# Two waits on GpSimd in a two-layer decoder: when the padded keys are zeroed, and when projection weights are split

## The reference, cut to what matters

```python
x = ln(x + hgrn(x, Wi, Wf, Wg, Wo, g_norm))                      # phase A
x = ln(x + cross_attention_one_head(x, ctx))                     # phase B
x = ln(x + experts_top2_of_8_width_64(x))                        # phase C
x = ln(x + causal_self_attention_16_heads(x, Wq, Wk, Wv, Wo))    # phase D
x = ln(x + causal_attention_16_heads_no_weights(x, ctx, ctx))    # phase E
x = ln(x + experts_top2_of_8_width_176(x) + shared_expert(x))    # phase F
```

## Time and profile before

| | us |
|---|---|
| median of 3 runs | 764.21 |
| lowest and highest | 762.01, 766.28 |
| span of the profiled execution | 762.5 |
| PE busy (share of the span) | 670.0 (88%) |
| DVE busy | 555.0 (73%) |
| POOL busy | 249.2 (33%) |

### The profile page before, as it was taken

How to read it: one execution, slowest core, us unless ns; L and a number is a source line. 1 busy time by engine, 2 the same in 40 slices (tenths; PEclk the granted TensorE clock), 3 DMA queues, 4 the chain that set the end, 5 groups by cost and what they waited for, 6 DMA issues and landing times.

```text
span 762.5 us, 18666 instructions
## 1 busy us (share of the span) xinstructions
PE 670.0 (88%) x4914; PEld 603.1 (79%) x4915; DVE 555.0 (73%) x2513; ACT 489.5 (64%) x1356; POOL 249.2 (33%) x420
## 2 busy tenths in 40 slices
PE   5889799858774888999999999999899979999982
PEld 5788578734443888999999999999899968888882
DVE  3788587767888546888898989998876735555474
ACT  4546566538772226999999999998555635555443
POOL 4343310133333700121212222222154625555651
PEclk9999899967885799999999999999999989999986
DMA  9960000000003387667776765661044423333175
GB/s 287 354 168 0 1 1 1 1 0 2 0 1 110 131 250 237 188 198 212 219 201 207 196 194 163 171 175 41 31 146 145 138 81 105 96 98 108 44 177 135
DMA packets 66488, 95.60 MB, mean 125 GB/s; under 512 B 11390, under 2 KB 52992, under 8 KB 66304
## 3 DMA queue, kind: packets, MB, share of 16 engines
q1 hardware_dynamic: 60912, 84.41, 38.0%
q0 software_dynamic: 5520, 10.53, 4.9%
HBM read 62.45 MB, written 33.36 MB: 126 GB/s over the span
## 4 chain that ended last, share of the span: by engine, by line
PE 39%; DVE 19%; issue 18%; DMA 11%; ACT 5%; POOL 4%; SPq 2%; DVEq 0%; POOLq 0%; ACTq 0%
PE bank L1955 9%; DMA xg<-X,idx 6%; PE bank L2106 6%; PE bank L1941 5%; PE bank L1687 4%; DVE bank L1406 3%; PE bank L2130 3%; PE bank L1930 3%; DVE smax L1406 2%; PE bank L2094 2%; PE bank L1971 2%; DMA late_mem<-yg 2%; DVE X L1151 1%; POOL rstd L625 1%; POOL xg L727 1%
## 5 line engine op out<-in xcount | busy, mean ns | idle before, releaser
L961 ACT ACTIVATE late_mem<-bank,smax 128x128 f32<-128x128 f32 x512 | 150.3, 409 | 15.3 <-DVE smax L1406 12.9
L1406 DVE CUSTOM_DVE_ANT_0 bank<-bank,causal 128x128 f32<-128x128 f32 x512 | 132.8, 322 | 17.7 <-issue 16.9
L1955 PE MATMUL bank<-f_mem,late_mem 128*128 128x68 f32 (+3 forms) x1024 | 127.8, 268 | 0.2
L1955 PEld LDWEIGHTS bank<-f_mem,late_mem 128*128 128x128 f32 x1024 | 124.6, 192 | 0.8 <-issue 0.5
L625 POOL TENSOR_TENSOR rstd<-var,power 128x2 f32<-128x2 f32 (+1 forms) x64 | 40.4, 632 | 189.7 <-DVE var L1144 178.2
L971 ACT ACTIVATE late_mem<-bank 128x512 f32<-128x512 f32 x128 | 82.6, 645 | 2.4 <-PE bank L1941 1.3
L1941 PE MATMUL bank<-ident,late_mem 128*128 128x128 f32 x512 | 78.4, 276 | 3.2 <-ACT late_mem L961 3.1
L1406 DVE DVE_READ_ACCUMULATOR2_ANT smax<- 128x1 f32 x512 | 71.8, 140 | 0.0
L1930 PE MATMUL bank<-kz,qs 128*128 128x256 f32 x256 | 63.8, 332 | 2.0 <-issue 0.9
L1941 PEld LDWEIGHTS bank<-ident,late_mem 128*128 128x128 f32 x512 | 59.2, 142 | 5.1 <-ACT late_mem L961 4.9
L2012 PE MATMUL bank<-x_hi,w_hi 128*128 128x256 f32 x176 | 51.0, 290 | 0.0
(11 more groups left out here) (285 smaller groups left out, 1991.8 us busy)
## 6 DMA issues: line engine op xcount, KB each, us to landing
qs<-q_D SPq DMA_DIRECT2D x64, 128.0 KB, 2.8
kz<-k_D SPq DMA_DIRECT2D x128, 64.0 KB, 2.6
qs<-q_E SPq DMA_DIRECT2D x64, 128.0 KB, 2.7
kz<-k_E SPq DMA_DIRECT2D x128, 64.0 KB, 2.5
xg<-f_mem SPq DMA_DIRECT2D x1, 5031.0 KB, 24.4
late_mem<-xg SPq DMA_DIRECT2D x39, 129.0 KB
q_D<-stage_d SPq DMA_DIRECT2D x8, 512.0 KB, 2.9
k_D<-stage_d SPq DMA_DIRECT2D x8, 512.0 KB, 3.9
```

Of the source, the lines that this page charges most:

```text
L961: ins = sc.activation(sp[:, g, i, :], bank[g][:, i * P:(i + 1) * P], ACT.Exp, bias=smax[:, g, i:i + 1], scale=-1.0)
L1406: ins = ve.tensor_tensor_reduce(v[:, i, :], v[:, i, :], causal[:, :], -1.0, 3e38, ALU.add, ALU.min, smax[:, g, i:i + 1])
L1955: ins = mm(bank[6][:, h * (DH + 1):to * (DH + 1)], spt[:, g, i, :], vf[:, slot, h:to, :].rearrange("p h d -> p (h d)"), start=True, stop=True)
```

## The change

POOL gets two more waits. Before the weight splits it waits for the eighth `c_copy` of phase B (`C_xs` 8), and before the zeroing of `kz` for the eighth `apply` of phase C (`ln_x` 24). No instruction is added, removed or resized, and no order within an engine changes.

```diff
             loaded(pool, "ld_d")
             pool.wait_ge(sem("B_o"), NU)
+            pool.wait_ge(sem("C_xs"), NU)
             for k, w in enumerate((sq, sk, sv)):
                 gp.tensor_copy(wd1_hi[:, k, :, :], w[:, :, :]).then_inc(sem("D_w"), 1)
                 pool.wait_ge(sem("D_w"), 2 * k + 1)
...
             pool.wait_ge(sem("C_o"), 2 * NU)
+            pool.wait_ge(sem("ln_x"), LN["D"])
             gp.memset(kz[:, :, :, :].bitcast(F32), 0.0).then_inc(sem("zeros"), 1)
             loaded(pool, "ld_e")
             for k in range(4):
```

## The result

Over 22 runs of each kernel the changed one takes 761.81 us (757.02 to 767.53) and the kernel before 766.18 (762.01 to 771.98): a ratio of 0.9945, 95% interval 0.9927 to 0.9963. That is 0.55% faster, 4.2 us. Forecast were 4.54 us, 0.59%. The median of before is now 2.0 us above that of the three runs on which the forecast of 759.7 us stood, so the ratio is the better witness of the two: the 761.81 us lie 2.1 us above the forecast time and 0.6 above its own range (758.2 to 761.2), inside the wider one (756.6 to 762.6).

A forecast was written before the change was run, and what follows sets the result against it. On the chain of waits, with PE busy 88%, DVE is shut out by POOL at two places. Terms 3.86 + 0.68 = 4.54 us off the 764.21 us median give 759.7 us; own range 758.2 to 761.2, 8 in 10 756.6 to 762.6.

The forecast's parts named there:

- The mechanism: Ends of phases B and C: DVE's scalings take 2.01 and 4.60 us instead of 0.74, shut out for POOL's whole instruction.
- Second wait: Seam of phases C and D: zeroing held until the scalings are done, so the first projection starts 3.86 us earlier.
- `d_x_low` beside a memset costs nothing: Seam of phases C and D: `d_x_low` isn't shut out by the moved zeroing; otherwise the price is 3.51 us.
- POOL's later end is hidden: After the zeroing's wait: memset and key splits end 0.9 us later, hidden; without that cover it would cost 0.9 us.
- First wait: End of phase B: weight splits wait, scalings and copy end 1.55 us earlier; 0.68 left after `top_two`'s first product is held.
- Phase C's pipeline then starts 0.68 us earlier as a whole: Start of phase C: what is left of the gain at phase B's end, 0.68 us, passes on whole.
- The clock's bounds: Phase D's first projections: PE's clock returning at once gains 2.4 us more; rising no earlier by the wall loses 1.7.
- The lag of 5.7 us: Phase D's projections: PE's clock rises some 5.7 us after PE begins again, taken as the same from the earlier start.
- the chain that moves as a whole: Phase D's projections: PE, ACT, DVE, SP's issues, a transfer and PE again, each link moving, so the 3.86 us arrives.
- Rival 5: Phase C: more turns at 10.50 instead of 8.70 us; from the third on slower, 765.1 us; chance 0.04.
- The wider range: Whole kernel: range for 8 in 10, 756.6 to 762.6 us, reaching to two clock rivals with half the scatter.
- rival 3: Phase D's projections begin earlier but the clock rises when it did: 2.8 us gained, 761.4 us; chance 0.12.

The follow-up runs named there:

- e4: Kernel before, without either new wait, with the zeroing of `kz` done twice in a row; ratio to the kernel before 1.0052 (1.0024 to 1.0080).
- e10: Repeat of e1, only the zeroing waits; ratio to the kernel before 0.9928 (0.9898 to 0.9958).
- e1: The change without the weight splits' wait, so only the zeroing waits; ratio to the kernel before 0.9975 (0.9953 to 0.9998).
- e5: The change, both waits kept, with the zeroing done twice in a row; ratio to the kernel before 0.9968 (0.9943 to 0.9993).
- e2: The change without the zeroing's wait, so only the weight splits wait; ratio to the kernel before 1.0006 (0.9980 to 1.0031).
- e8: The changed kernel itself, run again; ratio to the kernel before 0.9955 (0.9930 to 0.9980).
- e3: The change, with the third weight split moved behind DVE's `top_two` and gate arithmetic; ratio to the kernel before 0.9959 (0.9930 to 0.9987).
- e6: The change, plus 18 extra matmuls on PE before the first projection, results unused; ratio to the kernel before 0.9958 (0.9930 to 0.9986).
- e7: The change, with e3's later third split and e6's 18 extra matmuls; ratio to the kernel before 0.9920 (0.9889 to 0.9950).
- e11: Repeat of e2, only the weight splits wait; ratio to the kernel before 1.0009 (0.9985 to 1.0033).
- e12: Repeat of e7; ratio to the kernel before 0.9969 (0.9942 to 0.9997).
- e9: The change, with all three weight splits moved behind DVE's `top_two` and gate arithmetic; ratio to the kernel before 0.9912 (0.9876 to 0.9948), 7 runs.

## Why the prediction was right, step by step

The number is closer than its parts. Of the forecast 4.54 us, 3.86 were found where they were expected and 0.68 were not seen in the time; the measured 4.2 us have an interval of 2.8 to 5.6 us and can't tell 3.86 from 4.54.

- **The mechanism** (DVE is shut out by POOL's whole instruction): right, and shown by e4, each scaling behind its own memset.
- **Second wait, 3.86 us:** right to 0.01 us at the first projection (3.87), and it arrives: "attention" is 49.68 to 50.23 us in three profiles without the wait, 45.92 to 46.21 in six with it (45.44 in e10), and the mean ratio of e1 and e10, 0.995, is the change's.
- **`d_x_low` beside a memset costs nothing:** right, 1.28 us for two. This was the unknown with the widest bounds. The rule of the Trainium skill, "SBUF — State Buffer", section "Who interferes with whom", which the prediction set beside the row, holds here.
- **POOL's later end is hidden:** right; e5 puts 3.51 us more on it, and neither "PE" (2.20 us) nor "attention" (46.05) moves.
- **First wait, 0.68 us left of 1.55:** the size at the pick was nearly right (0.74), the product took 1.20 us where about 1.1 was forecast. The step that failed is the one after it: "Phase C's pipeline then starts 0.68 us earlier as a whole". It starts 0.44 us earlier (in e2 0.42), where PE's gap before the transposes grew and their second group ran at the low clock; and nothing of it is seen in the time (1.0006, 1.0009). The prediction priced the clock at the D seam and in phase C's turns, and missed it here.
- **The clock's bounds, from 2.4 us more to 1.7 us less:** too wide for what reaches the start of attention. The lag of 5.7 us that was carried over from the kernel before isn't fixed: one program shows 5.63 and 2.89. A rise 2.7 us earlier (e8 against the first profile) was given back behind the wait that SP's issues cause, which I took to be a part of the chain that moves as a whole. It does for the issues, but not for the clock.
- **Rival 5, slower turns of phase C:** "C" is 82.8 to 84.7 us in the four profiles without the splits' wait (before, e1, e4, e10; mean 83.5) and 83.0 to 85.5 in nine with it (the change, e2, e3, e5, e6, e7, e8, e11, e12; mean 84.8). The spread in each is as large as the difference. From the last inverse root of phase B to that of phase C it is 92.2 us on average without the wait (91.5 to 93.4) and 92.6 in the six profiles that have the wait as the change has it (91.0 to 93.5), so at that root the 0.74 us of the pick can't be found again. The sign that rival 5 named, more than one turn of 10.5 us, isn't there, but something near it is. The first four turns of phase C, from one inverse root to the next, take 8.63, 8.70, 10.53 and 8.69 us in the kernel before and 9.21, 8.70, 10.44 and 9.28 in the first profile of the change, 1.1 us more; in e8, the same program, they take 8.63, 8.70, 10.57 and 8.69. It may be that the wait loses a microsecond there, which would explain e2; it may be scatter. It isn't settled.
- **The wider range:** rival 3's 761.4 us with half the scatter of 1.5 us is 762.15, not the 762.6 that the prediction wrote; the time lies inside either.

So the 4.2 us are the zeroing's wait alone, as far as these times can tell. The other wait is worth nothing that could be measured. No version was shown to beat the change: e3, e6, e7 and e12 can't be told from it, and the interval of e9's better ratio overlaps the change's.

## What to carry to other kernels

Look at the duration of each DVE instruction against its fellows of the same form: one that is far longer than they are may not have worked longer but stood behind a GpSimd instruction, as each one shown here did; the row of that is then right beside it. A big GpSimd memset or cast that nobody needs soon belongs behind the last critical DVE instruction on SBUF, beside DVE work on PSUM; moving it costs one wait, and brought 3.9 us locally here. Then look at what it meets in its new place, with each DVE instruction that has two SBUF inputs, and at whether TensorE now waits longer somewhere behind it.

## What the runs showed of the hardware that was not expected

The engine that is shut out gets its turn even between two instructions that follow each other closely: in e4 DVE got exactly one instruction through between two memsets 0.06 us apart. An idle gap of PE that grew from 0.5 to 1.3 us or more went together with a second group of transposes at 1.02 instead of 0.72 us, at the low level of the clock (1.2 GHz), in six of six profiles; in five of them the clock had stayed there, in e5 it had risen and fell again. And one program's span outside the changed places can vary by more than the change: from the first softmax to the end it is 471.9 us in the changed kernel and 469.1 in e8, the same program, and 477.7 in e2 and 469.9 in e11, again the same.
